# Layer 1's W2 slab loads issued by GpSimd in place of SyncE, in a two-layer attention and FFN kernel on eight cores

## The reference

```python
xn = _layernorm(x, axis=-1)
x = x + _L0_attn_ref(xn, ...) + _L0_ffn_ref(xn, ...)     # layer 0
xn = _layernorm(x, axis=-1)
x = x + _L1_attn_ref(xn, ...) + _L1_ffn_ref(xn, ...)     # layer 1
```

```python
Wq1 = _quantize(W1)                  # [4096, 1024], values -1, 0, 1
Wq2 = _quantize(W2)                  # [1024, 4096]
h = jax.nn.relu(jnp.einsum('bsd,fd->bsf', x, Wq1) + b1)
out = jnp.einsum('bsf,df->bsd', h, Wq2) + b2
```

## Time and profile before

| | us |
|---|---|
| median of 3 runs | 1596.92 |
| lowest and highest run | 1594.79, 1741.78 |
| the profiled execution | 1601.35 |
| span of its slowest core (core 2) | 1599.8 |
| span of its fastest core (core 0) | 1573.6 |

### The profile page before, as it was taken

One profiled execution on the slowest core, in us unless ns is written; L12 is line 12 of the kernel. 1 busy time (PEld: TensorE's weight loads), 2 busy tenths in 40 slices (PEclk: granted clock), 3 DMA queues, 4 the chain that ended last, 5 costly groups with the idle time before them and its releaser, 6 DMA issues. The chain is left out here.

```text
span 1599.8 us, 15274 instructions; the slowest of 8 cores (1573.6 to 1599.8 us)
## 1 busy us (share of the span) xinstructions
PE 1238.0 (77%) x5332; PEld 536.2 (34%) x5440; DVE 418.8 (26%) x704; ACT 475.1 (30%) x550; POOL 140.6 (9%) x161
## 2 busy tenths in 40 slices
PE   0374289996796777755469499979997999889997
PEld 0121034442332323222124144434443444334443
DVE  2495435003323323333175200021002200031000
ACT  2463023334415526536023141013202140031400
POOL 3433100000101111112100000000000000000000
PEclk9987689997898888887779799989998999989999
DMA  9895952003426647566650654333434053231522
GB/s 196 128 161 79 142 72 50 1 0 105 117 69 210 191 125 238 157 211 196 128 96 1 158 145 132 118 132 110 154 116 148 28 151 138 93 118 48 182 109 109
DMA packets 74523, 194.43 MB, mean 122 GB/s; under 512 B 8496, under 2 KB 16720, under 8 KB 70096
## 3 DMA queue, kind: packets, MB, share of 16 engines
q1 hardware_dynamic: 41664, 121.65, 23.4%
q0 software_dynamic: 32784, 71.79, 22.2%
HBM read 195.57 MB, written 33.56 MB: 143 GB/s over the span
## 5 line engine op out<-in xcount | busy, mean ns | idle before, releaser
L1199 PE MATMUL pb<-bigA,wqA 128*128 128x512 bf16 x1002 | 225.2, 380 | 1.3 <-issue 0.2
L1159 PE MATMUL pb<-xn,xbf 128*128 128x512 bf16 x1004 | 221.5, 380 | 1.1
L1142 PE MATMUL pb<-stm,bigB 128*128 128x512 bf16 x627 | 144.8, 390 | 33.9 <-DVE xa_bf L1015 27.3
L1100 ACT ACTIVATE bigA<-pb,biasL,sc 128x512 bf16<-128x512 f32 x128 | 99.5, 777 | 219.2 <-PE pb L1159 219.2
L1181 PE MATMUL pb<-rt,projW 128*128 128x512 bf16 x501 | 126.5, 394 | 45.6 <-DVE rt L1020 39.7
L1050 DVE SCALAR_TENSOR_TENSOR xf<-pb,biasL,xf 128x512 f32<-128x512 f32 x32 | 24.0, 750 | 482.1 <-PE pb L1199 482.1
L1199 PEld LDWEIGHTS pb<-bigA,wqA 128*128 128x128 bf16 x1024 | 100.4, 98 | 121.6 <-issue 1.3
L1159 PEld LDWEIGHTS pb<-xn,xbf 128*128 128x128 bf16 x1024 | 100.2, 98 | 121.7
L1129 PE MATMUL pb<-xn 128*128 128x512 bf16 x313 | 79.6, 418 | 49.1 <-PEq L936 28.1
L681 PE MATMUL pb<-projW,xn 128*128 128x512 bf16 x503 | 112.0, 381 | 0.5
L1142 PEld LDWEIGHTS pb<-stm,bigB 128*128 128x128 bf16 x640 | 63.3, 100 | 115.3 <-issue 46.0
(11 more groups left out here) (135 smaller groups left out, 1104.8 us busy)
## 6 DMA issues: line engine op xcount, KB each, us to landing
xbf<-W1qS SPq DMA_DIRECT2D x128, 256.0 KB, 2.7
wqA<-W2qS SPq DMA_DIRECT2D x32, 1024.0 KB, 5.8
xbf<-W2T SPq DMA_DIRECT2D x26, 512.0 KB, 4.1
bigA<-W2T POOLq DMA_DIRECT2D x32, 256.0 KB, 9.3
bigA<-W1T POOLq DMA_DIRECT2D x16, 512.0 KB, 10.5
xf<-xT SPq DMA_DIRECT2D x4, 2048.0 KB, 8.5
x1S<-xf POOLq DMA_DIRECT2D x4, 2048.0 KB, 8.7
stm<-W1T SPq DMA_DIRECT2D x16, 512.0 KB, 5.0
```

Source lines behind the costliest of these rows:

```text
L1100: got = si(s.activation(bigA[:, fc * 512:(fc + 1) * 512], pb[fc % 2][:, :], AF.Relu, bias=biasL[:, 48 + fc:49 + fc], scale=sc[:, C_Q4:C_Q4 ...
L1142: got = ti(t.matmul(bank[:, :], bigB[:, i * 1024 + ec * 128: i * 1024 + (ec + 1) * 128], stm[:, i * 512:(i + 1) * 512], start=(n == 0), st ...
L1159: got = ti(t.matmul(bank[:, :], xbf[:, (fc % 4) * 1024 + dc * 128: (fc % 4) * 1024 + (dc + 1) * 128], xn[:, p0:p0 + TS], start=(dc == 0), ...
L1199: got = ti(t.matmul(bank[:, :], wqA[:, (dc % 2) * 4096 + fc * 128: (dc % 2) * 4096 + (fc + 1) * 128], bigA[:, fc * 512:(fc + 1) * 512], st ...
```

## The change

The eight loads of W2 slabs in each tile of layer 1 leave SP's queue and stand at the head of POOL's. The waits on `t_res[dc - 2]` go with them. They count on `sDi` and `sDj` in place of `sDc` and `sDd`, and PE waits for values that are computed ahead, since POOL's part of the program is written after PE's. A semaphore `sG` is made that nothing uses. Sizes, slots and the matmuls are as before.

```diff
@@ -939,6 +941,10 @@
             q_w2 = [0] * 8
             q_qld = [0] * 64
             q_qst = [0] * 64
+            if layer == 1:
+                w2q_q = [(qiD, sDi), (qjD, sDj)]
+                exp_w2 = [Q[["di", "dj"][dc % 2]] + 16 * (dc // 2 + 1)
+                          for dc in range(8)]
 
             @blk.sync
             def _(s):
@@ -972,14 +978,6 @@
                             xbf[:, (fc % 4) * 1024:(fc % 4) * 1024 + 1024],
                             bass.AP(W1qS.tensor, fc * 128 * 1024,
                                     [[1024, 128], [1, 1024]]))
-                    for dc in range(8):
-                        if dc >= 2:
-                            s.wait_ge(sT, t_res[dc - 2])
-                        sfn, _sh2 = store_q(dc)
-                        q_w2[dc] = sfn(s,
-                            wqA[:, (dc % 2) * 4096:(dc % 2) * 4096 + 4096],
-                            bass.AP(W2qS.tensor, dc * 128 * 4096,
-                                    [[4096, 128], [1, 4096]]))
 
             @blk.vector
             def _(v):
@@ -1173,7 +1171,7 @@
                     if dc >= 2:
                         t.wait_ge(sV, v_res[dc - 2])
                     if layer == 1:
-                        t.wait_ge(store_q(dc)[1], q_w2[dc])
+                        t.wait_ge(w2q_q[dc % 2][1], exp_w2[dc])
                     bank = pb[rb + dc % 2]
                     first = True
                     got = None
@@ -1206,6 +1204,15 @@
 
             @blk.gpsimd
             def _(g):
+                if layer == 1:
+                    for dc in range(8):
+                        if dc >= 2:
+                            g.wait_ge(sT, t_res[dc - 2])
+                        got = w2q_q[dc % 2][0](g,
+                            wqA[:, (dc % 2) * 4096:(dc % 2) * 4096 + 4096],
+                            bass.AP(W2qS.tensor, dc * 128 * 4096,
+                                    [[4096, 128], [1, 4096]]))
+                        assert got == exp_w2[dc], (dc, got, exp_w2[dc])
                 if layer == 0:
                     for h in range(NH):
                         if h >= 4:
```

More of the change, by code:

```diff
@@ L148, in build_nc @@
     sS = sem("sS")
+    sG = sem("sG")
     def _dma_track(key, semh, n0, inst):
```

## The result

The changed kernel takes 1600.46 us in the median of 42 runs, the kernel before 1596.39 us in the median of 42. The ratio is 1.002 with a 95% interval of 1.0012 to 1.0028: slower by 1.9 to 4.5 us. That is inside the range that was forecast and within 2%, but a gain of 1.3 us was expected, and the time moved the other way. (The ratios leave out runs in which one die ran at a lower clock than the other; the medians don't.) The middle of the interval is 3.2 us. The profiled execution took 1599.57 us; its slowest core is core 1, with 1597.8 us.

A forecast was written before the change was run, and what follows sets the result against it. Layer 1 was taken as bound by TensorE. Saving 0.84 us of wait and 1.7 of clock gave 1601.35 - 2.5 = 1598.8 us profiled; half, 1.3, off the median 1596.92 gave 1595.6 us, range 1591 to 1603.5.

The forecast's parts named there:

- the block's end isn't later either: End of layer 1's tiles: only outT's store stands behind POOL's waiting loads, and it waits for chunk 7 anyway; no cost.
- a transfer can only cost time where a matmul waits for it: Layer 1's tiles: TensorE bounds them, busy 646.9 of 690 us, so only matmul waits were searched for transfer costs.
- The wait of tile 0: Layer 1's first tile, chunk 0: the late W2 load costs up to 0.84 us, once, on three cores of eight.
- The 1.7 us of lost clock: Core 2, just after the first tile's late W2 load: TensorE's granted clock falls, losing 1.7 us, which the change would save.
- 4.7 us from issue to landing: W2 loads on POOL, chunks 2 to 7: estimated from outT's store; with 0.53 us ahead, 5.3 of 8.63 us, 3.3 spare.
- rival A: Layer 1, chunks 2 to 7: POOL's loads come late in every chunk, 55 us slower, 1692 us with clock; chance 0.05.
- Rival B: Start of layer 1's first tile: early W2 loads crowd W1 slabs, up to 4.7 us once, 1600 us; chance 0.12.
- Rival C: Whole kernel: no change, 1597 us; the slowest core had no late load, or the clock falls elsewhere anyway; chance 0.28.

The follow-up runs named there:

- before, again: The kernel before, unchanged, measured once more beside itself: ratio 1.0003 (0.9992 to 1.0014).
- The second comparison: The changed kernel, unaltered, measured once more beside the kernel before on the same chip: ratio 1.0008 (0.9990 to 1.0026).

## Why the prediction was wrong

**A loss of 1.4 us is shown, and where it arises.** The more transfers POOL has issued in a tile of layer 1 ahead of its store of outT, the later the next tile starts after that store, and a drain of POOL's queue at an earlier place takes the growth away. So POOL has something left to settle for each transfer, also for one that has long landed, and at the end of a block this stands behind the store, where nothing hides it. That the block's end is itself such a drain is inferred; no row names it.

| transfers of POOL's in the tile ahead of its store | store's issue to next start where it lands after 7.5, us | settling time, us |
|---|---|---|
| 0 (before, again, early on SP) | 7.84 to 7.91 | 0.38 |
| 2 | 7.96 to 8.00 | 0.49 |
| 6 | 8.14 to 8.17 | 0.64 |
| 8 (changed kernel, twice) | 8.20 to 8.24 | 0.72 |
| 24, of 512 bytes | 8.86 to 8.89, third passage 9.14 to 9.17 | 1.38 to 1.65 |
| 8, drained 18 us before the end | 7.88 to 7.92 | 0.39 |

That is 0.04 to 0.05 us each. The runs tell it from other causes: the number does it and not the bytes or the packets (24 small ones), not the loads' place in time (two early or six late), and a drain at a place where PE works takes it away. The price is 0.33 us at three passages and 0.38 at the end: 1.4 us on every core. Layer 1's length goes the same way, a mean of 696.3 us in two profiles of the changed kernel and 694.9 in two of the kernel before; but it is a coarse witness, as those two differ by 0.6 us, and with two loads on POOL it is already 695.8.

The price per transfer isn't a rule for every block. In layer 0 of the kernel before POOL issues 12 stores of W1 and W2 in the first tile, and 18 in the second and in the third, ahead of its store of x1S. On core 0 the settling times are 0.85, 0.61 and 0.60 us; by 0.04 each they would be 0.9, 1.1 and 1.1. Core 0 of the kernel before at the second passage of layer 0, timelines of POOL and SP, and the store's landing:

```profile
572.33 0.89 POOL L171 DMA_DIRECT2D x1S<-xf  x1 [9.39 <-DVE xf L1028]
...
580.44 0.38 SPq L171 DMA_DIRECT2D xf<-xT  x1
...
x1S<-xf POOLq DMA_DIRECT2D x1, 2048.0 KB, 7.5
```

Eighteen transfers cost less there than twelve, on all eight cores, and in layer 1 twenty-four cost more at the third passage than at the first two. What else sets the price was not found.

**The step that failed** is the sentence that "the block's end isn't later either". Its argument was that the last load has landed before chunk 7 begins. That is so (it is issued 18 us before the store and lands in 5), and it isn't enough: a load that has landed still costs the queue that issued it something at the block's end. The prediction asked what stands behind POOL's waiting loads in its queue and found the store alone. It left out the last thing in that queue, the end of the block, although it had found that 28.1 of PE's 43 us of idle in the stretch stand there. The same gap is in its sentence that a transfer can only cost time where a matmul waits for it: here the matmuls wait for the block's end, and that is later by 0.33 us.

**The gain was sized too high.** The working took the wait of tile 0 as usual and let half of the slowest cores have it. In the four profiles in which SP issues chunk 0's load behind the last W1 slab and nothing else disturbs tile 0 (before, again, six loads on POOL, the store on SP) a wait released by that load shows on 3, 0, 1 and 1 of eight cores, and two of these five are of 1.1 and 1.3 us, against the relu's 1.13, so they cost nothing or 0.2. Over the cores that is a mean of some 0.1 us. The 1.7 us of lost clock behind it stood on one core of one profile. So of the forecast 1.3 us some 0.1 was to be gained, and 1.4 to be paid. One profile can't say how often a wait occurs; all that could be read from it was that it is absent on five of eight cores.

**What was right.** POOL's loads: 4.7 us from issue to landing were expected, well inside the 8.63 of a chunk, and the trace has 4.9. This decides against rival A. Of the two figures of "DMA: Bandwidth & Descriptors" in the Trainium skill, the estimate of 4.4 us by the formula of its anatomy section is nearer to the 4.9 of the trace than the 6.15 us in the table of its section Bandwidth. Rival B did not come either: the first W1 slab on core 5 lands 13.2 us after its issue at 901.34, at 914.5, and PE takes it at 918.0. But the crowding is real, and little was spare: the first slab lands after 13.2 to 15.6 us on the eight cores where it took 7.9 to 10.4, and in three related kernels that load W2 early (two loads on POOL, early loads on SP, with the drain) one core each waits 0.3 to 0.6 us for a W1 slab in tile 0. Rival C, no change, was nearest, but for another reason than it gave.

**What stays open.** First, the size. The profiles explain 1.3 to 1.4 us; the 42 runs have 1.9 to 4.5. The second comparison, of 13 runs, has 1.0008 with an interval of -1.6 to 4.2 us and goes with both. So what the 42 runs have beyond 1.3 us isn't explained. The start of layer 1 on the slowest core doesn't differ: 902.6 and 901.0 us in the two profiles of the kernel before, 902.2 and 902.4 in those of the changed kernel. Second, the long landings. Two, one, one and one cores of eight have stores of outT that land after 8.1 us and more at all three passages in the four profiles in which POOL loads chunks 2 to 7 and stores outT (changed kernel, again, six loads, with the drain); in the five other kernels and profiles with that store on POOL none has (single stores reach 8.0 and, with the small transfers, 8.2). Layer 0 of the kernel before has them too: its stores of x1S, which follow POOL's stores of W1 and W2, land after 7.9 to 8.9 us at all of the passages on cores 2 and 5, partly so on 1 and 7, and after 7.5 on the other four. So, as far as these profiles show, they go with transfers that POOL issues in the last chunks before the store, and not with the W2 loads as such. The drain doesn't remove them. What makes a store's last bytes late on one core and not on the others was not found. Their cost isn't visible either: core 1 of the changed kernel has layer 1 in 695.6 us with them, core 5 in 696.3 without. A later start is partly paid back by the clock, at the one passage looked at. Stretch 1053 to 1058 on core 1, which starts its tile at 1055.28, and on core 5, which starts at 1053.71:

```profile
1053.00:1058.00 5.00, 2.72 (x7) 1.01 (x8) 2.72 (x12) 2.47 (x3) 1.06 (x2) 0.50 0.27 72
1058.00:1063.00 5.00, 5.00 (x22) 2.15 (x21) 2.31 (x4) 3.18 (x5) 0.00 (x0) 0.91 1.04 417
```
```profile
1053.00:1058.00 5.00, 4.29 (x11) 1.52 (x12) 3.77 (x13) 4.04 (x5) 1.06 (x2) 0.50 0.53 191
1058.00:1063.00 5.00, 5.00 (x22) 2.13 (x21) 1.53 (x3) 2.00 (x4) 0.00 (x0) 0.90 1.04 421
```

Both have half clock there and nearly full clock after. Core 5 works 1.57 us more of it at half clock, which is worth 0.8, and its time from the tile's start to its store is longer by just that, 158.90 against 158.09 us.

## What to carry to other kernels

A transfer that is moved to POOL's queue can cost more than its issue: in layer 1 POOL pays 0.04 us for each at the next end of a block (in two tiles of layer 0 less), and if the block ends on a transfer of POOL's, this comes on top of that transfer's landing, in front of all engines. Where the end of a block is the largest idle time of the busy engine, first ask which queue holds its last transfer: moving that one store from POOL to SP made the kernel 1.9% faster when done in layer 1 alone, and 3.5% when done in both layers with the moves of loads that went along, because the block's end waits for POOL's transfers and not for SP's, while the change that was studied moved work towards the queue that the block's end waits for. And how often a wait occurs has to be counted over cores and profiles before its removal is worth a number.

## What the runs showed of the hardware

- In layer 1 each transfer of POOL's ahead of its last store makes the next block start some 0.04 us later, whether it moves 512 bytes or 1 MB; a drain of POOL's queue while PE works removes this (0.72 to 0.39 us with eight).
- The end of a block waits until POOL's transfers have landed: PE idle 9.4 us with outT's store of 2 MB on POOL. With the store on SP it is 1.8 us, and the next tile's matmuls run while the store is under way.
- After an idle of 9.4 us at a passage TensorE's granted clock is 0.50 (1.2 GHz) for 5 to 6 us of the next tile; after an idle of 1.8 us it is 1.00 (2.4 GHz).
- Twenty-four transfers of 512 bytes (128 partitions of 4 bytes) ahead of a tile's loads moved the landing of the first four W1 slabs of 256 KB, behind 2 MB of xf, from 10.5 to 21.9 us after issue (median, core 4).
